# Routed experts of a decoder layer: blocks of two 64-row halves replaced by blocks of 128 rows of one expert

## What is computed

```
x = x + self_attention(layernorm(x))          # 16 heads, 4 key groups, rotary, sliding window of 64 plus sink
x = x + cross_attention(layernorm(x), ctx)    # 16 heads, causal
x = x + ffn(layernorm(x))
ffn:  shared = silu_and_mul(x @ Wgu.T) @ Wd.T * sigmoid(x @ sgate.T)          # hidden width 704
      p = softmax(x @ gate.T); the 4 largest of 16 experts per token, weights p
      routed = sum over those 4 experts e of p_e * (silu_and_mul(x @ w13[e].T) @ w2[e].T)   # width 176
      return shared + routed
```

## Time and profile before

| what | value |
|---|---|
| median of 3 runs | 402.02 us (398.63 to 402.61) |
| the profiled execution's own time | 403.16 us |
| its span, first to last instruction | 401.3 us |
| PE busy | 344.7 us (86%) |
| DVE, ACT, POOL busy | 227.7, 207.2, 178.8 us |
| moved by DMA | 72.54 MB |
| mean granted clock of TensorE | 0.933 |

### The profile page before, as it was taken

The page is one execution under the profiler, slowest core; times in us unless marked ns, Lnnn a source line. Parts: engine busy times, 40 slices in busy tenths (PEclk is TensorE's granted clock), DMA queues, the critical chain, the costliest instruction groups (busy, mean ns, idle before and its releaser), DMA issues.

```text
span 401.3 us, 7934 instructions
## 1 busy us (share of the span) xinstructions
PE 344.7 (86%) x2362; PEld 217.5 (54%) x2378; DVE 227.7 (57%) x688; ACT 207.2 (52%) x557; POOL 178.8 (45%) x212
## 2 busy tenths in 40 slices
PE   6988899999999978789996697897796888789893
PEld 2446576766777755477774343443443444346672
DVE  3387689889896899533725233333243333343884
ACT  1265688788897568344331354454344444552221
POOL 5481315343360516670664344655465455443000
PEclk9899899999999999758996599999899899999998
DMA  7997995979889452120682325554454455452931
GB/s 222 302 282 223 426 278 154 275 224 274 224 222 271 130 159 80 43 109 29 254 331 72 116 86 155 159 154 154 125 182 138 144 159 154 136 164 91 361 111 53
DMA packets 41747, 72.54 MB, mean 181 GB/s; under 512 B 5346, under 2 KB 29042, under 8 KB 40562
## 3 DMA queue, kind: packets, MB, share of 16 engines
q1 hardware_dynamic: 35490, 56.08, 46.5%
q0 software_dynamic: 5376, 15.13, 11.2%
q10 hardware_dynamic: 848, 0.92, 0.9%
HBM read 40.58 MB, written 31.53 MB: 180 GB/s over the span
## 4 chain that ended last, share of the span: by engine, by line
PE 40%; DVE 20%; issue 13%; ACT 10%; another core or an unknown queue 7%; POOL 5%; DMA 4%; ACTq 0%; DVEq 0%; POOLq 0%; SPq 0%
PE bank L1719 10%; ACT probs L656 6%; PE bank L1459 6%; PE bank L1741 5%; DVE neg_max L917 5%; PE bank L1731 3%; DVE probs_t L923 2%; PE bank L1381 2%; PE bank L1373 2%; PE bank L1429 2%; PE bank L1402 2%; PE bank L1604 1%; POOL y_picks L603 1%; PE bank L1709 1%
## 5 line engine op out<-in xcount | busy, mean ns | idle before, releaser
L1719 PE MATMUL bank<-w,xbt 128*64 x160 | 58.0, 489 | 20.4 <-ACT xbt L787 15.5
L656 ACT ACTIVATE probs<-bank,neg_max 128x128 f32<-128x128 f32 x256 | 69.9, 416 | 6.2 <-DVE neg_max L917 5.1
L603 POOL DMA_INDIRECT y_picks<-yb,ids x40 | 39.3, 982 | 51.9 <-DVE yb L1265 44.7
L1721 PE MATMUL bank<-w_odd,xbt 128*64 128x352 f32 x160 | 58.1, 489 | 0.0
L1258 DVE TENSOR_TENSOR hb<-sg,bank 128x176 f32<-128x176 f32 x40 | 13.5, 338 | 71.5 <-ACT sg L795 29.3
L611 POOL DMA_INDIRECT xb<-x_slots,rows x40 | 38.5, 962 | 21.8 <-DVE ids L1274 8.7
L1719 PEld LDWEIGHTS bank<-w,xbt 128*64 128x64 f32 x160 | 21.8, 144 | 44.6 <-issue 37.5
L795 ACT ACTIVATE sg<-bank 128x176 f32<-128x176 f32 x40 | 12.7, 317 | 63.8 <-PE bank L1721 43.0
L543 POOL DMA_INDIRECT x_slots<-x,slots x32 | 32.3, 1009 | 27.5 <-DVE slots L1046 19.5
L917 DVE TENSOR_REDUCE neg_max<-bank 128x4 f32<-128x512 f32 x64 | 41.5, 683 | 5.3 <-PE bank L1373 4.6
L1743 PE MATMUL bank<-w_odd,hbt 128*64 128x256 f32 x160 | 43.8, 398 | 0.0
(11 more groups left out here) (181 smaller groups left out, 740.5 us busy)
## 6 DMA issues: line engine op xcount, KB each, us to landing
x_slots<-zero_b SPq DMA_DIRECT2D x16, 1072.0 KB, 11.1
w_odd<-w_in_dram SPq DMA_DIRECT2D x40, 256.0 KB
w<-w_in_dram SPq DMA_DIRECT2D x4, 1408.0 KB, 12.0
w<-w_in_dram SPq DMA_DIRECT2D x4, 1024.0 KB
yg<-y_picks SPq DMA_DIRECT2D x8, 512.0 KB, 7.0
ktc<-keys_d SPq DMA_DIRECT2D x16, 192.0 KB
sw_raw<-shared_in_dram SPq DMA_DIRECT2D x6, 384.0 KB, 3.4
keys_d<-ctxt_h SPq DMA_DIRECT2D x4, 512.0 KB, 6.8
```

The source lines that it names most:

```text
L603: pool.indirect_dma_start(y_picks[:, :], bass.IndirectOffsetOnAxis(ids[:, n:n + 1], 0), yb[:, n % RB, :], None).then_inc(yb_placed[n % RB] ...
L656: ins = act.activation(probs[:, g, j, :], ps_s[g][:, 128 * j:128 * j + 128], ACT.Exp, bias=neg_max[:, g, j:j + 1])
L1719: pe.matmul(ps_gu[n % 2][0:ROWS, 0:GU], xbt[:, n % 2, k, 0:ROWS], w13[:, bass.ds(experts[n], 1), k, :].rearrange("p e n -> p (e n)"), star ...
L1721: ins = pe.matmul(ps_gu[n % 2][ROWS:128, 0:GU], xbt[:, n % 2, k, ROWS:128], w13_odd[:, n % 2, k, :], start=k == 0, stop=k == KC - 1)
```

## The change

A block now holds 128 rows of one expert. There are 47 blocks instead of 40, since an expert's last block may now waste up to 127 rows. The rows of a block lie one behind the other in `x_slots`, so SP brings them with an ordinary DMA whose address comes from a register (`load_rows`); POOL keeps only `place_rows`. The down weights of a block are loaded by SP from DRAM into one of four buffers, and nothing else of `w2` is in SBUF. `w13_odd`, `w2_odd`, `copy_up` and the load of the whole of `w2` are gone. PE multiplies all 128 rows at once: `block_up` and `block_down` are half as many matmuls of 128 columns instead of 64. PE reads eight packed words instead of seven. SP's loop issues `load_rows(n + 5)` and then `load_down(n + 3)`.

```diff
-ROWS = 64
-NBLK = -(-((B * T * TOPK + NE * (ROWS - 1)) // ROWS) // 2)
-RW = 3
+NBLK = (B * T * TOPK + NE * 127) // 128
...
-        w13_odd = place("w13_odd", [128, 2, KC, GU])
-        w2_odd = place("w2_odd", [128, RW, KC, D])
-        w2 = place("w2", [128, NE, KC, D])
+        w2 = place("w2", [128, RB, KC, D])
...
+            def load_rows(n):
+                if n >= RB:
+                    sp.wait_ge(xbt_psum, n - RB + 1)
+                    sp.wait_ge(ids_ready, n - RB + 1)
+                row = sp.value_load(table[0:1, NBLK + n:NBLK + n + 1], min_val=0, max_val=EMPTY)
+                sp.dma_start(xb[:, n % RB, :], x_slots[bass.ds(row, 128), :]).then_inc(xb_loaded[n % RB], 16)
+
             def load_down(n):
-                if n >= RW:
-                    sp.wait_ge(yb_psum, n - RW + 1)
+                if n >= RB:
+                    sp.wait_ge(yb_psum, n - RB + 1)
                 e = sp.value_load(table[0:1, n:n + 1], min_val=0, max_val=NE - 1)
-                sp.dma_start(w2_odd[:, n % RW, :, :].rearrange("p k d -> p (k d)"),
-                             w2_in[:, bass.ds(e, 1), :, :].rearrange("p e k d -> p (e k d)")).then_inc(w2_odd_loaded[n % RW], 16)
+                sp.dma_start(w2[:, n % RB, :, :].rearrange("p k d -> p (k d)"),
+                             w2_in[bass.ds(e, 1)].rearrange("e p k d -> p (e k d)")).then_inc(w2_loaded[n % RB], 16)
 
             sp.wait_ge(x3_ready, B)
-            for i in range(4):
-                es = slice(4 * i, 4 * i + 4)
-                sp.dma_start(w2[:, es, :, :], w2_in[:, es, :, :]).then_inc(w2_loaded, 16)
             sp.wait_ge(table_ready, 3)
+            for n in range(RB - 1):
+                load_down(n)
+            sp.wait_ge(scattered, 16 * TOPK * B)
+            for n in range(RB + 1):
+                load_rows(n)
             for n in range(NBLK):
-                load_down(n)
+                if n + RB + 1 < NBLK:
+                    load_rows(n + RB + 1)
+                if n + RB - 1 < NBLK:
+                    load_down(n + RB - 1)
...
-            def gather_rows(n):
...
             for n in range(NBLK):
-                if n + RB < NBLK:
-                    gather_rows(n + RB)
-                if n:
-                    place_rows(n - 1)
-            place_rows(NBLK - 1)
+                place_rows(n)
...
-            copy_up(0)
-            copy_up(1)
             take_rows_t(0)
             take_rows_t(1)
             block_gate(0)
-            copy_up(2)
...
-                if n + 3 < NBLK:
-                    copy_up(n + 3)
...
-            pe.wait_ge(table_ready, 2)
+            pe.wait_ge(table_ready, 3)
...
-                pe.wait_ge(w13_odd_ready, n + 1)
+                e = experts[n]
                 for k in range(KC):
-                    pe.matmul(ps_gu[n % 2][0:ROWS, 0:GU], xbt[:, n % 2, k, 0:ROWS],
-                              w13[:, bass.ds(experts[n], 1), k, :].rearrange("p e n -> p (e n)"), start=k == 0, stop=k == KC - 1)
-                    ins = pe.matmul(ps_gu[n % 2][ROWS:128, 0:GU], xbt[:, n % 2, k, ROWS:128], w13_odd[:, n % 2, k, :],
-                                    start=k == 0, stop=k == KC - 1)
+                    ins = pe.matmul(ps_gu[n % 2][:, 0:GU], xbt[:, n % 2, k, :],
+                                    w13[:, bass.ds(e, 1), k, :].rearrange("p e n -> p (e n)"), start=k == 0, stop=k == KC - 1)
...
-                pe.wait_ge(w2_odd_loaded[n % RW], 16 * (n // RW + 1))
+                pe.wait_ge(w2_loaded[n % RB], 16 * (n // RB + 1))
...
                 for k in range(KC):
-                    pe.matmul(ps_yb[n % 2][0:ROWS, 0:D], hbt[:, n % 2, k, 0:ROWS],
-                              w2[:, bass.ds(experts[n], 1), k, :].rearrange("p e n -> p (e n)"), start=k == 0, stop=k == KC - 1)
-                    ins = pe.matmul(ps_yb[n % 2][ROWS:128, 0:D], hbt[:, n % 2, k, ROWS:128], w2_odd[:, n % RW, k, :],
-                                    start=k == 0, stop=k == KC - 1)
+                    ins = pe.matmul(ps_yb[n % 2][:, 0:D], hbt[:, n % 2, k, :], w2[:, n % RB, k, :], start=k == 0, stop=k == KC - 1)
...
-            pe.wait_ge(w2_loaded, 64)
```

More of the change, by code:

```diff
@@ L44 @@
 WORDS = -(-NBLK // PACK)
-NEXP = WORDS * PACK
 EMPTY = NE * REGION
@@ L96, in decoder_layer @@
         tri = place("tri", [128, 2, 128], BF16)
[L97 to L100, removed]
+        upto = place("upto", [NE, NE + 128 + NBLK])
+        dump = place("dump", [128, NBLK])
         of_block = place("of_block", [128, NBLK])
@@ L135, in decoder_layer @@
         counts_i = place("counts_i", [NE, 2], I32)
-        after = place("after", [NE, 2, 2 * NEXP])
-        table = place("table", [1, NBLK], I32)
-        words = place("words", [1, 2 * WORDS], I32)
+        after = place("after", [NE, NBLK])
+        table = place("table", [1, 2 * NBLK], I32)
+        words = place("words", [1, WORDS], I32)
         ex = place("ex", [128, B, NE])
@@ L152, in decoder_layer @@
         cursor[0] = shared_at
-        packs = place("packs", [1, 2 * NEXP])
-        packed_f = place("packed_f", [1, 2 * NEXP])
-        words_f = place("words_f", [1, 2 * WORDS])
+        ends = place("ends", [1, 2, 2, NBLK])
+        packs = place("packs", [1, WORDS * PACK])
+        packed_f = place("packed_f", [1, WORDS * PACK])
+        words_f = place("words_f", [1, WORDS])
+        table_f = place("table_f", [1, 2 * NBLK])
         cursor[0] = after_shared
@@ L357, in decoder_layer @@
         xb_loaded = [sem(f"xb_loaded{r}") for r in range(RB)]
-        w2_loaded = sem("w2_loaded")
-        w2_odd_loaded = [sem(f"w2_odd_loaded{r}") for r in range(RW)]
-        w13_odd_ready = sem("w13_odd_ready")
+        w2_loaded = [sem(f"w2_loaded{r}") for r in range(RB)]
         yb_placed = [sem(f"yb_placed{r}") for r in range(RB)]
@@ L803, in take_hidden_t @@
                                ACT.Copy).then_inc(hbt_ready, 1)
-            act.wait_ge(table_ready, 2)
-            packed = [act.value_load(words[0:1, WORDS + i:WORDS + i + 1], min_val=0, max_val=NE ** PACK - 1) for i in range(WORDS)]
-            number = act.alloc_register("expert_odd")
-            def copy_up(n):
-                act.reg_alu(number, packed[n // PACK], 4 * (n % PACK), ALU.logical_shift_right)
-                act.reg_alu(number, number, NE - 1, ALU.bitwise_and)
-                e = act.snap(number, min_val=0, max_val=NE - 1)
-                if n >= 2:
-                    act.wait_ge(gu_psum, n - 1)
-                act.activation(w13_odd[:, n % 2, :, :], w13[:, bass.ds(e, 1), :, :].rearrange("p e k n -> p (e k) n"), ACT.Copy
-                               ).then_inc(w13_odd_ready, 1)
-            act.wait_ge(w13_loaded, 64)
-            act.wait_ge(x2_ready, B)
-            copy_up(0)
-            copy_up(1)
             take_rows_t(0)
@@ L1172, in block_table @@
                 dve.tensor_copy(words[:, :], words_f[:, :]).then_inc(table_ready, 1)
-                dve.tensor_scalar(table[:, :], ps_t[0:1, first + NEXP:first + NEXP + NBLK], float(NE - 1), None, ALU.min
-                                  ).then_inc(table_ready, 1)
-                dve.tensor_scalar(of_block[:, :], ps_t[:, TABLE_AT:TABLE_AT + NBLK], float(NE - 1), None, ALU.min
-                                  ).then_inc(table_ready, 1)
             def gated(n):
@@ L1572, in block_table @@
             def block_table():
-                pe.wait_ge(after_ready, 2)
-                for part in range(2):
-                    at = TABLE_AT + NBLK * part
-                    for i in range(2):
-                        pe.matmul(ps_t[ROWS * i:ROWS * i + ROWS, at:at + NBLK], upto[:, NE:NE + ROWS],
-                                  after[:, part, i:2 * NBLK:2], start=True, stop=True)
-                at = TABLE_AT + 2 * NBLK
-                for i in range(2):
-                    ins = pe.matmul(ps_t[0:1, at + NEXP * i:at + NEXP * i + NEXP], upto[:, NE:NE + 1], after[:, 0, i::2],
-                                    start=True, stop=True)
-                ins.then_inc(table_psum, 1)
+                pe.wait_ge(after_ready, 1)
+                pe.matmul(ps_t[:, TABLE_AT:TABLE_AT + NBLK], upto[:, NE:NE + 128], after[:, :], start=True, stop=True)
+                pe.matmul(ps_t[0:1, TABLE_AT + NBLK:TABLE_AT + 2 * NBLK], counts[:, 1:2], after[:, :], start=True, stop=True
+                          ).then_inc(table_psum, 1)
             def rows_of(n):
```

51 lines of the change are left out of this document (22 added, 29 removed).

## The result

The change is faster: 382.06 us (median of 4, 381.12 to 384.40) against 400.32 us (397.97 to 402.61) for the kernel before on the same chip, a ratio of 0.955 (95% interval 0.947 to 0.964). I had forecast 413.9 us and slower. The profiled execution took 384.4 us, its span is 382.5. Every profile here is of one execution, and that of the kernel before is of one of its slower ones (403.16 us, where its median was 394.8 to 401.6 on the chips of the experiments), so a loop time taken from the profiles can be some us off where a ratio of whole times is not.

A forecast was written before the change was run, and what follows sets the result against it. PE was the first suspect, 86% busy, with ACT's chain next after the change. Loop 119.6 + 3.1 + 21.3 = 144.0 us, +11.2, plus 0.65 at the start: 415.0 us profiled, 413.9 median; range 391 to 422.

The forecast's parts named there:

- late signals: Block loop: PE's signals reaching ACT 1 to 2 us late in some blocks, cause unknown; kept at 21.3 us.
- Rival B: Late signals tied to POOL's indirect DMAs, falling to 13.4 us as 73 become 46; 406.0 us in all, chance 0.14.
- Rival A: Late signals go away, as PE pauses every block and all products have one shape; 392.6 us in all, chance 0.27.
- under 130 us, the late signals were tied to the two-half form: Sign set beforehand: a loop time this short would show that products on two 64-row halves caused the late signals.
- low clock: Block loop: two short slices at a granted clock near 0.6, kept at 3.1 us.
- end: Stage after the loop, last blocks' results and second half of the shared network; claimed not to change.
- 46 intervals: Block loop: 47 blocks instead of 40, at 2.60 us each, 119.6 us against 108.4 for 39 at 2.78.
- start of the loop: Before the first block: PE reads eight words instead of seven, +0.65 us; a further 0 to 2 us taken as 0.
- chain through ACT: Block loop: PE, ACT, PE from one up product to the next, claimed to set the period at 2.60 us.
- PE's up product should show idle time before it in nearly every block: Sign set beforehand: PE would wait briefly in the loop because ACT sets the pace.
- PE's work: Per block 2.53 us; halving the matmuls saves nothing, some 0.25 us goes where 64-column and 128-column work meet.
- rival C: Late signals come per block with nothing covering them, or PE's 0.25 us gaps stay; about 422 us, chance 0.08.

The follow-up runs named there:

- e3: The kernel after with one unused GpSimd gather of 128 rows per block put back, into spare buffers; ratio 1.062 to the kernel before, loop 151.4 us.
- e6: The kernel after with each block's scatter issued twice, the second to a spare buffer; ratio 1.070 to the kernel before, loop 153.8 us.
- e11: The kernel after with a spare GpSimd gather of 16 rows in every block; ratio 1.062 to the kernel before, loop 152.2 us.
- e5: The kernel after with a spare plain GpSimd load of 128 fixed rows per block instead of a gather; ratio 0.953 to the kernel before, loop 113.7 us.
- e7: The kernel after with a spare plain load of 134 KB per block on ScalarE's queue; 382.7 us, no ratio given, loop 113.7 us.
- e1: The kernel after with PE's products back on two 64-row halves, 47 blocks, part of the computation left out; ratio 0.988 to the kernel before.
- e2: The kernel before with products over all 128 rows, second half's expert left out, gathers and copies kept; ratio 1.002 to the kernel before, loop 128.1 us.
- e9: The kernel before, complete, its gathers replaced by plain loads, half the rows by SP and half by GpSimd; ratio 0.945, loop 107.1 us.
- e8: The kernel before, complete, its rows brought by SP in two plain loads of 64 rows per block; ratio 1.063, loop 155.2 us.
- e4: The kernel after with the routing's expert-counting product widened from 16 to 128 columns; ratio 0.954 to the kernel before, loop 113.6 us.
- e12: The kernel before with plain loads by SP and GpSimd for its gathers, plus one GpSimd wait moved ahead in the routing; ratio 0.943, loop 107.4 us.
- e10: The kernel after with a spare GpSimd gather in every second block only; ratio 0.981 to the kernel before, loop 122.3 us.

## Why the prediction was wrong

**The step that failed** is "For the late signals ... I take them as they are now, 21.3 us". They are 0 after. Their cause is the second indirect DMA of GpSimd per block, two before and one after: adding one brought them back (e3, e6, e11), a plain DMA in its place didn't (e5), traffic didn't (e7), the form of the products neither made nor cured them (e1, e2), and replacing the gathers alone in the kernel before removed them (e9). My reason for keeping them, "since the stage's length and its engines stay about the same", looked at busy engines and not at what the change takes from GpSimd's queue.

Rival B had the cause, from the right observation (delays only where GpSimd issues them; there is one where attention overlaps with the routing too, which I had missed: DVE's L1002 at 179.25 waits 1.1 us beyond the end of PE's product at 178.17, in a row of scatters), but I priced it in proportion, 13.4 us for 46 of 73, and so above what would have made it faster. In the runs one per block costs 0 (PE is idle 0.6 us of the loop), one and a half 8.5 us, two 38 to 40 us. Rival A had the effect, but its reasons (PE's pauses, one shape) are refuted: the kernel after pauses less, and halves aren't late either. So is the sign that I had set for it, "under 130 us, the late signals were tied to the two-half form": e1 has the halves, takes 126.5 us and has no late signal. Even A's sum, 403.16 less 9.5 for the profiled execution, was 9.3 us too long: it kept the period of 2.60 (5.9 us), the low clock (3.1) and the start (1.8), and took the end 1.5 too short.

**The terms, one by one** (profiled execution, forecast 415.0, measured 384.4):

| term | forecast | measured |
|---|---|---|
| late signals | 21.3 | 0 |
| low clock in the loop | 3.1 | 0 (clock 1.00) |
| 46 intervals | 119.6 (2.60 each) | 113.7 (2.50 each, the last ones shorter) |
| start of the loop | 232.3 | 230.5 |
| end | 36.8 | 38.3 |

The period was mis-sized. PE's own sum, 2.53, was nearly right, and the chain through ACT, which I made the bound at 2.60, isn't one: from a first up product to the Silu it is 1.40 (299.47 to 300.87), then 0.50 to ACT's L777 at 301.37, and 0.60 to the next product at 301.97, of which I had said 0.52 is needed. With 0.52 that chain takes 2.42 us, 0.08 less than PE's own 2.50, and PE hardly stands. "PE's up product should show idle time before it in nearly every block" is false: 0.6 us in all.

**PE's work.** The 0.25 us at the meetings of 64 and 128 columns went, as forecast; e1 brings them back as 0.28, which over 46 intervals is 12.8 us (the part of rival C that would have been true without the wider products). The Trainium skill, "TensorEngine Tiling (Array Packing)", section Tiling Modes, has the mode switch drain the engine. This case's traces agree in that time is lost at both changes, 0.28 us per block for the one to the narrow form and the one back together; a drain as such is not in the profile.

**Rows by SP** cost nothing, as forecast: the transfer takes 2.32 us, and the steps of the register reads keep their 152 and 18 ns. SP's bound exists, but at three issues (e8). **Start:** PE waited for its words as forecast, and the rows were there before. The late signal in the routing stayed, so the load of `w2` isn't its cause. That the loop begins 1.8 us earlier than I said is no merit of the change as far as the profiles show: the ranks' products end 2.6 us earlier already (202.87 against 205.50), and over the fourteen profiles they end anywhere between 200.7 and 208.8. From there to the loop it is 27.7 us, 1.5 more than before and not 0.65. **End:** 38.3 instead of 36.8 us, where the granted clock was 0.89 instead of 0.96. **ACT's copies** and their removal were worth nothing, as forecast: e9 keeps them all at 2.79 us.

**What the change is made of.** The loops of before, e9, e1 and after lead from one kernel to the other: gathers off GpSimd 132.8 to 107.1, minus 25.7 us; 47 blocks instead of 40, plus 19.4 (e1, 126.5); products over 128 rows, minus 12.8 (113.7). The 19.4 are seven blocks at e1's 2.78. All of the gain comes from the first step, and the other two together cost 6.6 us. The ratios of the whole times, which don't hang on single profiles, give the same order: 0.945 for e9, 0.988 for e1, 0.955 for the change. e9, without the last two steps, is the faster kernel by its loop, and by about 1% in the ratios (0.945 and 0.943 against 0.953 to 0.955 for the change and its harmless variants); the intervals overlap, so the order of the two is likely and not proved.

**Open:** what in an indirect DMA of GpSimd holds up the signals and the small steps of other engines. No run separates the issue on GpSimd from the handling of its descriptors. With one and a half per block on average there is harm already; whether it is their number or that two stand side by side isn't shown, for no run spaces two of them apart. That the mean granted clock of the loop was below 1.00 wherever the up product's signals were late is seen in the profiles, and what lowered it isn't tested.

## What to carry to other kernels

When signals between two engines come late by 1 us or more and neither is to blame, look at GpSimd's queue at that moment: here two indirect DMAs within 2.5 us did it, to engines that had no part in them, and one did not. Rows that lie one behind the other need no gather; a plain load with its address in a register, on SyncE or GpSimd, did no such harm here, but count SyncE's issues per block. And when a change removes one of a resource's two users, price the disturbance they cause together at zero as well as in proportion.

## What the runs showed of the hardware

- Indirect DMAs of GpSimd at one per 2.50 us disturbed nothing (loop 113.7 us), three per 5 us cost 8.5 us, two per 2.5 us 38 to 40 us over 47 blocks, with 16 rows as with 128. A row of scatters every 1.26 us held a signal of PE back by 4.1 to 5.7 us, until after its last one.
- The disturbance reached SP's register steps: 18 ns became up to 679, 152 up to 703 (e3).
- Three DMA issues with a register address per block kept SP busy 3.98 us (e8); two fitted into 2.50 (after).
- The granted clock was 1.00 in the loops in which PE hardly waited (after, e1, e4, e5, e7, e9, e12: 0.6 to 0.7 us of idle time), also 1.00 in e10 with 6.3 us, and 0.92 to 0.97 in those in which it was idle 19.9 us or more (before, e2, e3, e6, e11, and e8 without a late signal). I had counted 3.1 us of low clock as fixed.
